# A fused decoder block on one core: batch 0's mixer and batch 1's projections computed in float32r pieces, in another block order

## What is computed

```python
xn = x * rsqrt(mean(x * x) + EPS) * w_norm            # after a layer norm
proj = einsum('bld,td->blt', xn, W_in)                # 2576 outputs of 512 inputs
z, xi, dt, Bm, Cm = split(proj, [1024, 1024, 16, 256, 256])
xi = silu(causal_conv4(xi, w_conv))
dt = softplus(dt + dt_bias); dA = exp(dt * -exp(A_log))
x_mean = xi.reshape(b, l, 16, 64).mean(-1)
u = (dt * x_mean)[..., None] * Bm
h = dA_t * h + u_t; y_t = sum(h * C_t)                # scan over 512 tokens
y = einsum('blh,ih->bli', y, W_h2i) * silu(z)
out = einsum('bli,di->bld', y, W_out) + residual
```

## Time and profile before

| what | us |
|---|---|
| median of three runs | 1204.52 (1203.93 to 1207.58) |
| profiled execution, its own time | 1203.86 |
| span of that execution in the trace | 1202.1 |
| TensorE busy | 1153.5 (96%) |
| VectorE busy | 764.6 (64%) |
| ScalarE busy | 519.7 (43%) |
| GpSimd busy | 389.2 (32%) |

### The profile page before, as it was taken

How to read it: one execution, slowest core, us unless ns; L and a number is a source line. 1 busy time by engine, 2 the same in 40 slices (tenths; PEclk the granted TensorE clock), 3 DMA queues, 4 the chain that set the end, 5 groups by cost and what they waited for, 6 DMA issues and landing times. The chain is left out here.

```text
span 1202.1 us, 31773 instructions
## 1 busy us (share of the span) xinstructions
PE 1153.5 (96%) x13278; PEld 599.5 (50%) x13280; DVE 764.6 (64%) x1244; ACT 519.7 (43%) x716; POOL 389.2 (32%) x502
## 2 busy tenths in 40 slices
PE   5999999999999999999999999999999999999996
PEld 3444434444545544544555654454444555555554
DVE  3833596756788575659666687877848555555553
ACT  3321224533555453455444365555543244444443
POOL 5212311221321230131122123111101477777776
PEclk9999999999999999999999999999999999999998
DMA  9320795104175310356410136310105876788740
GB/s 208 102 82 22 185 179 113 37 16 120 48 155 96 85 33 2 94 103 132 85 55 16 31 104 105 72 44 4 73 3 186 231 152 139 192 237 235 194 82 13
DMA packets 119605, 122.26 MB, mean 102 GB/s; under 512 B 25472, under 2 KB 84992, under 8 KB 119344
## 3 DMA queue, kind: packets, MB, share of 16 engines
q1 hardware_dynamic: 101744, 98.59, 32.2%
q0 software_dynamic: 17008, 21.16, 9.3%
q10 hardware_dynamic: 720, 0.61, 0.2%
HBM read 94.63 MB, written 40.77 MB: 113 GB/s over the span
## 5 line engine op out<-in xcount | busy, mean ns | idle before, releaser
L684 DVE TENSOR_REDUCE mx<-ps_m 128x2 f32<-128x1024 f32 x256 | 312.8, 1222 | 193.6 <-PE ps_m L1025 189.4
L893 ACT ACTIVATE prob<-ps_s 128x1024 f32<-128x1024 f32 x256 | 261.9, 1023 | 322.9 <-PE ps_s L1025 322.0
L1025 PE MATMUL acc<-xnT,wring 128*32 128x512 f32 x1888 | 249.4, 593 | 0.6 <-DVE first_z L620 0.6
L1915 PE MATMUL ps_gu<-ring,xgT 128*128 x376 | 176.9, 593 | 1.5 <-DVE xgT L1590 1.0
L1525 POOL DMA_INDIRECT out<-y,dest x92 | 146.3, 1590 | 61.0 <-ACT y L1776 41.2
L1025 PE MATMUL ps_s<-q_stack,k_stack 99*32 99x512 bf16 x2048 | 161.8, 380 | 4.4 <-ACT prob L893 3.8
L1025 PE MATMUL ps_m<-k_stack,q_stack 96*32 96x512 bf16 x1952 | 153.3, 380 | 9.7 <-DVE mx L684 8.1
L1210 PEld LDWEIGHTS ps_o<-prob,values 128*32 128x32 f32 x4096 | 116.4, 110 | 44.6 <-issue 39.1
L1210 PE MATMUL ps_o<-prob,values 128*32 128x128 f32 x4096 | 138.5, 273 | 0.0
L1025 PEld LDWEIGHTS ps_m<-k_stack,q_stack 96*32 96x32 bf16 x1952 | 55.9, 96 | 127.1 <-issue 72.4
L1708 DVE TENSOR_TENSOR down_low<-ring,down_high 128x1024 fp32r<-128x1024 f32 x46 | 56.3, 1225 | 66.6 <-ACT down_high L1762 66.6
(11 more groups left out here) (291 smaller groups left out, 1391.0 us busy)
## 6 DMA issues: line engine op xcount, KB each, us to landing
ring<-in_w_experts SPq DMA_DIRECT2D x96, 256.0 KB, 5.4
wring<-in_w_in SPq DMA_DIRECT2D x80, 256.0 KB, 4.3
q_stack<-part_rows SPq DMA_DIRECT2D x96, 128.0 KB, 4.8
wring<-in_w_out SPq DMA_DIRECT2D x32, 256.0 KB, 2.8
part_rows<-part SPq DMA_DIRECT2D x20, 384.0 KB, 4.0
out<-x SPq DMA_DIRECT2D x4, 1024.0 KB, 4.8
xt<-in_x SPq DMA_DIRECT2D x14, 256.0 KB, 4.4
k_stack<-part_rows SPq DMA_DIRECT2D x48, 64.0 KB, 3.2
```

What stands on the lines that cost most here:

```text
L684: nc.vector.tensor_reduce(mx[:, n % G, 2 * u:2 * u + 2], ps_m[:, :, :], AX.X, ALU.max).then_inc(s_max, 1)
L893: nc.scalar.activation(prob[:, slot % PROB, :, :], ps_s[:, :, :], ACT.Exp, scale=SCALE).then_inc(s_exp, 1)
L1025: ins = nc.tensor.matmul(dst[c:c + 32, :], stationary[:, c:c + 32], moving, start=start, stop=stop, tile_position=(0, c))
L1915: ins = nc.tensor.matmul(ps_gu[p][:, :], xgT[:, p, k * P:(k + 1) * P], weights(own)[:, k * 2 * F:(k + 1) * 2 * F], start=(k == 0), stop=(k ...
```

## The change

For batch 0's whole mixer and for the 20 projection blocks of batch 1 (`SPLIT_BATCHES = 2`) each operand is cut into a float32r piece that holds its high bits and a second piece with the rest, and a product is three float32r matmuls: high by high, high by low, low by high (`split_product`). The rest of the kernel keeps float32 products.

- **Pieces.** ScalarE copies each loaded weight block to its high piece (`high_weights`), GpSimd subtracts to get the low one (`low_weights`), 48 blocks in all. The transposed activations are evacuated as a high piece by ScalarE (`evacuate_high`, 16 instructions of 128x128 per batch) and a low piece by VectorE (`evacuate_low`, also 16). In batch 0 the gated channels get pieces too (`high_gated`, `low_gated`, eight each).
- **Weights.** The 10 places of the ring become 5 pairs, so only five blocks are in flight until the last split block; a block's high and low piece are made three and four slots after the load is asked for (`HIGH_AT`, `LOW_AT`).
- **Order.** In batches 0 and 1 the xi blocks come first (n = 1 to 8), then B and C (9 to 12), then z; dt moves from m = 0 to m = 18, and takes two products in place of one since its moving operand has two pieces. `head_means` moves to m = 25 and 26, u to m = 32.
- **Silu.** xi's silu is one ScalarE activation in batches 0 and 1 and z's in batch 0; VectorE has no part in these. `w_h2i`'s pieces are cut by ScalarE and VectorE instead of GpSimd.
- **Banks.** Batch 1 has four PSUM banks up to block 12. The transposes of its tokens go to `ps_m` and `ps_o` between the `heads_to_inner` products.
- **Out.** `project_out` of batch 0 runs over the weight block first and the token tile second, and all four `x1` tiles are added at m = 59 to 62. `statistics` and `residual` of the next batch move (`NEXT_AT`, `REST_AT`), and products in slots 0 to 13 are not tiled.

```diff
-    RING = 10
+    RING = 5
...
-    PROB = 6
+    PROB = 4
     N = B * G
-    K_AT = -47
+    K_AT = (-44, -47, -47, -47)
...
-    TURN_AT = (50, 52, 58, 60)
+    TURN_AT = ((43, 44, 45, 55), (50, 52, 58, 60), (50, 52, 58, 60))
+    EVAC_AT = ((50, 51, 52, 56), (50, 52, 58, 60), (50, 52, 58, 60))
...
-    Y_AT = (40, 38, 38, 38)
+    Y_AT = (38, 38, 38, 38)
+    XI = [tuple(range(1, 9))] * 2 + [tuple(range(5, 13))] * 2
+    BC = [tuple(range(9, 13))] * 2 + [tuple(range(1, 5))] * 2
+    DT_AT = (18, 18, 0, 0)
+    MEANS_AT = (25, 26, 30, 30)
+    U_AT = (32, 32, 34, 34)
+    NEXT_AT = (22, 30, 4, 4)
+    REST_AT = ((28, 29, 30, 31), (36, 38, 40, 42), (9, 9, 10, 10))
+    KEEP_AT = (7, 9, 11, 13)
+    ORDER = (0, 2, 4, 6, 1, 3, 5, 7)
+    SPLIT_BATCHES = 2
     KHALF_AT = (-32, 1)
...
+        xnT_high = sb("xnT_high", [P, KD, SEQ], F32R)
+        xnT = over("xnT", [P, KD, SEQ], F32)
+        xnT_low = sb("xnT_low", [P, KD, SEQ], F32R)
...
+        def out_order(b):
+
+            if b:
+                return [(j, q) for j in range(TB) for q in range(KI)]
+            return ([(j, q) for q in range(KI - 2) for j in range(TB)]
+                    + [(j, q) for j in range(TB) for q in (KI - 2, KI - 1)])
+
+        def consumed(b, w):
+
+            if w < GROUPS - 1:
+                return s_proj, (GROUPS - 1) * b + w + 1, 2 * w + 4
+            q = w - GROUPS + 1
+            at = (OUT_AT + out_order(b).index((TB - 1, q))) // 2 + 1
+            if q == KI - 1:
+                return s_out, TB * (b + 1), at
+            return s_wout, (KI - 1) * b + q + 1, at
+
...
+        HIGH_AT = {w: freed_at(w - RING) + 3 for w in range(RING, FIRST_RAW)} | {23: 42, 24: 49}
+        LOW_AT = {w: at + 1 for w, at in HIGH_AT.items()} | {23: 42, 24: 50}
...
+        X1_AT = ((59, 60, 61, 62), (50, 54, 58, 62), (50, 54, 58, 62), (50, 54, 58, 62))
+        CUT_AT = (25, 26, 27, 28, 29)
...
+        def turn(b, n):
+
+            if b >= SPLIT_BATCHES or n > KI:
+                return n
+            return n - 1 if n else KI
+
+        def place(b, n):
+
+            if b == 0:
+                return turn(b, n) % 4
+            if b == 1 and n <= 12:
+                return (turn(b, n) + 1) % 4
+            return (b + n) % 2
...
+            def low_weights(w):
+
+                pool.wait_ge(s_whigh, w + 1)
+                nc.gpsimd.tensor_tensor(pieces[:, w % RING, 1, :], landed(w), pieces[:, w % RING, 0, :],
+                                        ALU.subtract).then_inc(s_wlow, 1)
...
+            def evacuate_low(b, j):
+
+                dve.wait_ge(s_xhigh, TB * b + j + 1)
+                turned = turn_bank(b, j)
+                for k in range(KD):
+                    cols = slice(j * P, (j + 1) * P)
+                    ins = nc.vector.scalar_tensor_tensor(
+                        out=xnT_low[:, k, cols], in0=turned[:, k * P:(k + 1) * P], scalar=wnorm[:, k, 0:1],
+                        in1=xnT_high[:, k, cols], op0=ALU.mult, op1=ALU.subtract)
+                ins.then_inc(s_xnT, 1)
...
+            def evacuate_high(b, j):
+
+                act.wait_ge(s_tr, TB * b + j + 1)
+                turned = turn_bank(b, j)
+                for k in range(KD):
+                    ins = nc.scalar.activation(xnT_high[:, k, j * P:(j + 1) * P], turned[:, k * P:(k + 1) * P],
+                                               ACT.Copy, scale=wnorm[:, k, 0:1])
+                ins.then_inc(s_xhigh, 1)
+
+            def high_weights(w):
+
+                act.wait_ge(s_raw[w % RING], 16 * (w // RING + 1))
+                nc.scalar.activation(pieces[:, w % RING, 0, :], landed(w), ACT.Copy).then_inc(s_whigh, 1)
...
-                    if m >= 29 and m % 2 == 1 and (m - 29) // 2 < 7:
+                    if m % 2 == 0 and m // 2 - 1 in XI[b]:
+                        taps(b, XI[b].index(m // 2 - 1))
+                    if b and m >= 29 and m % 2 == 1 and (m - 29) // 2 < 7:
                         silu_z(b, (m - 29) // 2)
-                    if m >= 15 and m % 2 == 1 and (m - 15) // 2 < KI:
-                        silu_xi(b, (m - 15) // 2)
-                    if m == 31:
...
+                    if m % 2 == 0 and m // 2 - 2 in XI[b]:
+                        i = XI[b].index(m // 2 - 2)
+                        act.wait_ge(s_conv, KI * b + i + 1)
+                        if b < SPLIT_BATCHES:
+                            nc.scalar.activation(xz[:, i, :], xz[:, i, :], ACT.Silu).then_inc(s_xs, 1)
...
+                            if i == 2:
+                                act.wait_ge(s_mean, 1)
+                            nc.scalar.activation(gated[i], bank(b, 13 + i), ACT.Silu).then_inc(s_zs, 1)
...
+            def split_product(dst, stationary, moving, start, stop):
+
+                nc.tensor.matmul(dst, stationary[0], moving[0], start=start, stop=False)
+                nc.tensor.matmul(dst, stationary[0], moving[1], start=False, stop=False)
+                return nc.tensor.matmul(dst, stationary[1], moving[0], start=False, stop=stop)
...
-                w = BLOCKS * b + n - 1
                 if k == 0:
                     bank_free(b, n)
-                    pe.wait_ge(s_w[w % RING], 16 * (w // RING + 1))
-                weights = ring[:, w % RING, k * P:(k + 1) * P]
-                ins = product(bank(b, n), weights, xnT[:, k, :], start=(k == 0), stop=(k == KD - 1))
+                    weights_there(b, n - 1)
+                weights, cols = weights_of(b, n - 1), slice(k * P, (k + 1) * P)
+                if b < SPLIT_BATCHES:
+                    ins = split_product(bank(b, n), [w[:, cols] for w in weights],
+                                        (xnT_high[:, k, :], xnT_low[:, k, :]), start=(k == 0), stop=(k == KD - 1))
+                else:
+                    ins = product(bank(b, n), weights[:, cols], xnT[:, k, :], start=(k == 0), stop=(k == KD - 1))
...
-                if at == 0:
+                if at == 2 * DT_AT[b]:
                     project_steps(b)
-                elif 4 <= at < 4 * GROUPS:
```

More of the change, by code:

```diff
@@ L135, in stream_phase @@
         gated = [first_z[:, 0, :], first_z[:, 1, :]] + [xz[:, i, :] for i in range(2, KI)]
+        gated_low = [first_z_low[:, 0, :], first_z_low[:, 1, :]] + [xz_low[:, i, :] for i in range(2, KI)]
         q = xz[:, TB:, :]
@@ new lines, in load_block, with load_raw, load_whole @@
+                sp.dma_start(dst.rearrange("p (k c) -> p k c", k=KD), dram["w_in"][:, :, col:col + P]
+                             ).then_inc(done, 16)
+            def load_raw(w):
+                load_block(landed(w), *divmod(w, BLOCKS), s_raw[w % RING])
+            def load_whole(r):
+                b, w = divmod(FIRST_RAW + r, BLOCKS)
+                load_block(ring[:, unit(r), :], b, w, s_whole[unit(r)])
+            def freed(b, w):
+                done, value, _ = consumed(b, w)
+                this = BLOCKS * b + w
+                sp.wait_ge(done, value)
+                if this >= FIRST_RAW:
+                    if this + 2 * RING < BLOCKS * B:
+                        load_whole(this - FIRST_RAW + 2 * RING)
+                elif this + RING >= FIRST_RAW:
+                    for i in range(2):
+                        load_whole(2 * (this + RING - FIRST_RAW) + i)
+                else:
+                    load_raw(this + RING)
@@ L328, in _ @@
             sp.dma_start(wdt[:, :, 0:H], dram["w_in"][:, :, O_DT:O_DT + H]).then_inc(s_head, 16)
[L329 to L332 removed]
+            for w in range(RING):
+                load_raw(w)
             load_keys(0)
@@ L562, in statistics, with variances @@
                     steps.n += 1
-            def variances(b):
+            def variances(first, last):
                 dve.wait_ge(s_v, steps.n)
-                for j in range(TB):
+                for j in range(first, last):
                     ins = nc.vector.bn_aggr(mv[:, j, :], st[:, j, :])
                 steps.then(ins)
-                steps.then(nc.vector.tensor_scalar(var_eps[:, :, 0], mv[:, :, 1], LN_EPS, None, ALU.add))
-                nc.vector.scalar_tensor_tensor(out=var_eps[:, :, 1], in0=var_eps[:, :, 0], scalar=RMS_EPS,
-                                               in1=mv[:, :, 1], op0=ALU.mult, op1=ALU.add).then_inc(s_ve, 1)
+                part = slice(first, last)
+                steps.then(nc.vector.tensor_scalar(var_eps[:, part, 0], mv[:, part, 1], LN_EPS, None, ALU.add))
+                nc.vector.scalar_tensor_tensor(out=var_eps[:, part, 1], in0=var_eps[:, part, 0], scalar=RMS_EPS,
+                                               in1=mv[:, part, 1], op0=ALU.mult, op1=ALU.add).then_inc(s_ve, 1)
             def inverse(b):
-                dve.wait_ge(s_rs, b + 1)
+                dve.wait_ge(s_rs, b + 2)
                 nc.vector.tensor_scalar(keep[:, :, 0], rstd[:, :, 0], 1.0, None, ALU.add)
@@ L787, in last_group @@
                 nc.vector.tensor_scalar(last_ve[:, :], last_mv[:, :, 1], LN_EPS, None, ALU.add).then_inc(s_lve, 1)
-            for j in range(TB):
```

(30 more changed lines are left out.)

480 lines of the change are left out of this document (291 added, 189 removed).

## The result

| what | before | after |
|---|---|---|
| median | 1206.07 us (1203.40 to 1208.73, 8 runs) | 1196.24 us (1194.82 to 1200.73, 8 runs) |
| profiled execution, span | 1202.1 us | 1194.3 us |

The account below looks back on a forecast made before the run. TensorE, busy for 96% of the span, bounds the kernel. 31.1 - 2.0 - 1.4 + 4.7 + old waits (5.9 + 1.0 + 0.3) - new waits (3.8 + 5.2 + 3.5) = 27.1 us off 1203.86: 1177 us, range 1165 to 1189.

Parts of the forecast that it names:

- Products, -31.1: Three float32r matmuls of 0.232 us make each of 192 split products 0.696 us in place of 0.858: 31.1 us less.
- dt, 2.0: With two moving pieces dt takes 2.0 us where it was spaced 1.0: 2.0 us more over two batches.
- Start, 1.4 later at 17.0: High and low pieces of the first activations let the first block start near 17.0 us, 1.4 later.
- The chain in batch 0, 3.8: From dt at m = 18 to y takes 35.5 us; TensorE reaches the outputs at 31.7 and waits 3.8.
- heads_to_inner, 3.4: One round of gates, copies and pieces takes 3.4 us; first weights to first out product were 7.2: 4.7 less.
- Batch 1 up to slot 0: Old waits of 5.9 us go; queries, first query stack, row maxima and two taps bring 5.2 us of new ones.
- the checkpoints: Listed signs of being right, among them first out product near 86, slot 0 near 161 and slot 14 near 204.
- Slots 0 to 13, 3.5 of new waits: VectorE gets batch 2's statistics and residuals, 36.0 us of work beside TensorE's 39.3: 3.5 us of new waits.
- they come twice: Rival: new waits are twice as large, through DMA load and ScalarE waiting for landings; 14 to 20 us gained; chance 0.20.
- the last paragraph: Listed signs of being wrong: ScalarE's high pieces waiting for landings with TensorE idle, wider triples, or changes after slot 14.
- The rest as before, 971: After slot 14 the same instructions run on TensorE's time, so that stretch stays as long as before, 971 us.

Follow-up runs that it names:

- Experiment 5: Changed kernel's order and pieces kept, but each of the 192 products is one float32 matmul on the high pieces: 1214.06 us, ratio 1.0069 to the kernel before.
- Experiments 2 and 6: Residual of batch 1 moved later in the changed kernel: 1198.79 us; dt of batch 0 first, decay at m = 21, with later stack transfers: 1185.71 us.
- The control: Changed kernel with only one register operation more before each wait for expert weights: 1195.87 us, ratio 0.9913 to the kernel before.

## Why the prediction was wrong

The direction and the size of the work were right. The sum failed in its waits, and in a term that it did not have. By its own steps:

- *Products, -31.1.* Right: 0.233 a matmul, 2.79 a block. Experiment 5 shows that the kernel gets 18.2 of it. Why a float32r matmul takes 0.233 where a bf16 one of the same columns takes 0.215, no run shows.
- *dt, 2.0.* Right: 40.79 to 42.75.
- *Start, 1.4 later at 17.0.* It was 16.25, but with 1.9 more at half clock: 1.1 worse.
- *The chain in batch 0, 3.8.* TensorE waited 3.5 for pieces and 3.2 (by spacing) before the outputs: 2.9 worse. The chain ended 39.1 us after dt in place of 35.5. The gain came on time (58.9; I had 58.5). What failed is the landing: I let u follow the gain's spread and forgot that the decay's spread, now issued after it, had to land too (73.97). Experiments 2 and 6 show it. That a low piece can be held for 4.6 us was not in the sum either.
- *heads_to_inner, 3.4.* 4.55 us; the first low piece of VectorE took 1.35 us, where I had 0.7, beside a gate of GpSimd. The 7.2 us that I started from were partly at half clock (0.50 from 93.1 to 96.5), which I did not see.
- *Batch 1 up to slot 0.* 78.8 us where the checkpoints had 75. The queries' wait was 3.3, not 1.2: the four `first_q` took 3.81 us beside two low pieces of GpSimd, where the earlier trace rows have 0.5 each. Behind it came 1.7 at half clock. The first query stack had landed in time, and the other waits together were as forecast.
- *Slots 0 to 13, 3.5 of new waits.* The step that failed most: 50.2 us in place of 43. I counted VectorE's load there and not what stands in SyncE's queue before a weight load. The rival "they come twice" named the mechanism, ScalarE waiting in order for a landing with copies behind it, and gave it 0.20; the last paragraph named it as a sign of being wrong. The sum had no place for it. It took 4.9 us, and the clock 2.9. The measured time is outside that rival's 1184 to 1190 too. All else in the stretch was 0.6 better than forecast.
- *The rest as before, 971.* 973.5 from slot 14's scores on: 1.6 of half clock and 0.9 more of waits in slots 14 and 15. The control's execution had no half clock there.

Sum against the forecast of 1177: 5.9 to the first out product (5.2 of it in the steps above), 3.8 to slot 0, 7.2 to slot 14 and 2.5 after it, 19 us. Across these, 8.1 us are the clock (1.9 + 1.7 + 2.9 + 1.6), a term that the prediction did not have. The kernel before had no pause of 3 us in this part, and its one half-clock stretch went unread.

## What to carry to other kernels

When the bounding engine gets faster, look for waits where an in-order queue holds a landing in front of work that it needs: list the transfers ahead of each load at the new pace, and move those that nobody reads soon. Price a pause of TensorE of about 3 us at its length plus 1.7 to 2.9 us for the clock, which came behind most such pauses here and not behind all; a cluster of short waits can bring it as well. Read the granted clock of the kernel before in windows of a few us ahead of pricing a stage. Where a chain ends in several landings, sum each of them, not the one that was last before.
